# A graph layer and a mixture of experts on one core: the lane columns of the first message list on GpSimd, the second list earlier

## What is computed

```
x = x + gnn(layernorm(x))                     # x: 625 x 512
    h_self = n @ W_self.T + b_self
    H[r]   = n @ W_rel[r].T + b_rel[r]        # r in 0..15, two for each of the 8 relations
    agg[heads] += H[rel, tails]; agg[tails] += H[rel + 8, heads]
    gnn    = relu(h_self + agg)
x = x + moe(layernorm(x))                     # 16 experts, the best 2 for each token
```

## Time and profile before

| what | value |
|---|---|
| median of three runs | 734.15 us |
| the profiled execution, its own time | 737.15 us |
| its span, first to last instruction | 735.4 us |
| TensorE busy | 695.0 us (95%) |
| VectorE busy | 617.0 us (84%) |
| ScalarE busy | 500.8 us (68%) |
| GpSimd busy | 307.4 us (42%) |
| mean granted TensorE clock | 0.98 |
| graph layer, from the trace | 0 to about 404 us |

### The profile page before, as it was taken

How to read it: one execution, slowest core, us unless ns; L and a number is a source line. 1 busy time by engine, 2 the same in 40 slices (tenths; PEclk the granted TensorE clock), 3 DMA queues, 4 the chain that set the end, 5 groups by cost and what they waited for, 6 DMA issues and landing times. The chain is left out here.

```text
span 735.4 us, 10603 instructions
## 1 busy us (share of the span) xinstructions
PE 695.0 (95%) x3210; PEld 546.5 (74%) x3210; DVE 617.0 (84%) x1204; ACT 500.8 (68%) x717; POOL 307.4 (42%) x279
## 2 busy tenths in 40 slices
PE   4999989999998989999997899999999999999993
PEld 4777766777776767777765688888888888888882
DVE  8899978997997757777775899999998999999990
ACT  3555466774675757877556498888877888888860
POOL 3000077752777577776771033322234223333201
PEclk9999999999999999999999899999999999999997
DMA  8347588884988888997767989999999999999932
GB/s 244 124 143 270 176 264 293 302 273 149 305 288 275 268 288 273 302 310 211 226 203 252 353 318 349 398 407 394 401 369 369 367 402 372 363 395 372 371 106 29
DMA packets 54436, 212.75 MB, mean 289 GB/s; under 512 B 9753, under 2 KB 10150, under 8 KB 39158
## 3 DMA queue, kind: packets, MB, share of 16 engines
q1 hardware_dynamic: 34998, 153.85, 55.5%
q0 software_dynamic: 19392, 58.35, 27.3%
HBM read 184.36 MB, written 27.80 MB: 289 GB/s over the span
## 5 line engine op out<-in xcount | busy, mean ns | idle before, releaser
L400 POOL DMA_INDIRECT rows_sb<-h_dram,row_of x190 | 210.9, 1110 | 170.4 <-DVE row_of L544 83.8
L554 DVE TENSOR_TENSOR rows_lo<-rows_sb,rows_hi 128x512 fp32r<-128x512 f32 x175 | 119.8, 685 | 53.6 <-ACT rows_hi L692 53.3
L825 PE MATMUL p_h<-g_hi_sb,xt_hi_whole 128*125 128x512 f32 x320 | 129.6, 405 | 1.1 <-ACT p_h L686 0.8
L826 PE MATMUL p_h<-g_lo_sb,xt_hi_whole 128*125 128x512 f32 x320 | 127.6, 399 | 0.0
L827 PE MATMUL p_h<-g_hi_sb,xt_lo_whole 128*125 128x512 f32 x320 | 127.5, 398 | 0.0
L692 ACT CAST rows_hi<-rows_sb 128x512 fp32r<-128x512 f32 x175 | 99.2, 617 | 29.3 <-DMA rows_sb<-h_dram,row_of 27.1
L677 ACT COPY h_whole<-p_h 125x512 f32<-125x512 f32 x80 | 46.9, 586 | 89.9 <-PE p_h L827 89.9
L1190 POOL DMA_INDIRECT tokens<-token_dram,rows_of_tokens x15 | 21.7, 1444 | 171.2 <-ACT rows_of_tokens L1479 131.9
L859 PE MATMUL p_sum<-rows_hi,seg_hot 128*125 128x512 f32 x175 | 72.7, 416 | 8.6 <-DVE rows_lo L554 8.2
L1243 DVE TENSOR_TENSOR u_lo_sb<-stage_up,u_hi_sb 128x2048 fp32r<-128x2048 f32 x34 | 76.4, 2285 | 1.0
L1243 DVE TENSOR_TENSOR d_lo_sb<-stage_down,d_hi_sb 128x2048 fp32r<-128x2048 f32 x32 | 71.8, 2286 | 3.1 <-ACT d_hi_sb L1464 3.0
(11 more groups left out here) (291 smaller groups left out, 1308.8 us busy)
## 6 DMA issues: line engine op xcount, KB each, us to landing
stage_up<-in_L_ffn_up_w SPq DMA_DIRECT2D x34, 1024.0 KB, 8.2
stage_gate<-in_L_ffn_gate_w SPq DMA_DIRECT2D x32, 1024.0 KB, 8.7
stage_down<-in_L_ffn_down_w SPq DMA_DIRECT2D x32, 1024.0 KB, 7.7
h_dram<-h_whole SPq DMA_DIRECT2D x80, 224.0 KB
stage_up<-in_L_gnn_W_rel SPq DMA_DIRECT2D x16, 1024.0 KB, 8.0
x_whole<-in_L_gnn_b_rel SPq DMA_DIRECT2D x16, 256.0 KB, 9.5
rows_sb<-h_dram,row_of POOLq DMA_INDIRECT x190, 4.9
h_dram<-h_whole SPq DMA_DIRECT2D x80, 26.0 KB
```

The source lines that it names most:

```text
L400: q.indirect_dma_start(rows_sb[:, b % ROWS], None, h_dram[0:1 + made(n) * TP], bass.IndirectOffsetOnAxis(ap=row_of[:, b:b + 1].bitcast(U32 ...
L554: v.tensor_tensor(rows_lo[:, b % PARTS], rows_sb[:, b % ROWS], rows_hi[:, b % PARTS].bitcast(F32), ALU.subtract).then_inc(part_lo, 1)
L825: m.matmul(o, xt_hi[:, dc, at], wt_hi_sb[:, 1 - j % 2, dc], start=(by_matmul and dc == 0), stop=False, skip_group_check=True)
L826: m.matmul(o, xt_hi[:, dc, at], wt_lo_sb[:, 1 - j % 2, dc], start=False, stop=False, skip_group_check=True)
```

## The change

1. GpSimd makes the 85 `lane_hot` columns of list 0, in a loop that stands between its constants and its first gather. Ahead of it is a wait on a new semaphore, `placed`, which VectorE increments when `lane[:, d]` is made. GpSimd waits for `list_taken` as VectorE does, and increments `lanes_made` once for each five columns.
2. VectorE leaves `lane_hot` out for list 0 and makes `told_hot` alone.
3. TensorE's `list_chunk` waits for `lanes_made` too, for list 0.
4. The table of columns changes. List 0: 6.5 columns a product from i = 4. List 1: 5 a product in 19 to 22, 1.5 in 23 to 37, 6 in 38 to 42, 2 from 43. `told_of(1)` and `places(1)` move three products ahead, to i = 17 and 18.

```
-LISTS = ((4, 5.5), (24, 3))
+LISTS = (((4, 18, 6.5),), ((19, 23, 5), (23, 38, 1.5), (38, 43, 6), (43, 58, 2)))
...
+        placed, lanes_made = sem("placed"), sem("lanes_made")
...
-                begin, each = LISTS[d]
-                return max(0, min(EC, int(each * (i - begin))))
+                n = 0
+                for begin, end, each in LISTS[d]:
+                    n += each * (max(begin, min(i, end)) - begin)
+                return min(EC, int(n))
...
                 pool.wait_ge(spare_cleared, 64)
+                pool.wait_ge(placed, 1)
+                for c in range(EC):
+                    n, k = c // HOT, c % HOT
+                    if k == 0 and n >= HOT_SETS:
+                        pool.wait_ge(list_taken, n - HOT_SETS + 1)
+                    i = q.tensor_scalar(lane_hot[:, n % HOT_SETS, k], slot_iota[:], lane[:, 0, c:c + 1], None, ALU.is_equal)
+                    if k == HOT - 1:
+                        i.then_inc(lanes_made, 1)
                 for b in range(BLOCKS):
...
-                    v.scalar_tensor_tensor(lane[:, d], nth, -float(P), place, ALU.mult, ALU.add)
+                    v.scalar_tensor_tensor(lane[:, d], nth, -float(P), place, ALU.mult, ALU.add).then_inc(placed, 1)
...
-                    v.tensor_scalar(lane_hot[:, n % HOT_SETS, k], slot_iota[:], lane[:, d, c:c + 1], None, ALU.is_equal)
+                    if d:
+                        v.tensor_scalar(lane_hot[:, n % HOT_SETS, k], slot_iota[:], lane[:, d, c:c + 1], None, ALU.is_equal)
...
-                    if i == 20:
+                    if i == 17:
                         told_of(1)
...
-                    if i == 21:
+                    if i == 18:
                         places(1)
...
                     pe.wait_ge(list_hot, nth + 1)
+                    if d == 0:
+                        pe.wait_ge(lanes_made, n + 1)
```

More of the change, by code:

```diff
@@ L142, in build @@
         round_sems = range(steps.num, logits_full.num + 1)
-        assert len(round_sems) == 54 + OUTS + BIAS_ROWS
+        assert len(round_sems) == 56 + OUTS + BIAS_ROWS
         ln2_stored, gap_ready, exp_ready = sem("ln2_stored"), sem("gap_ready"), sem("exp_ready")
```

## The result

The changed kernel takes **746.86 us**, the median of 4 runs (745.60 to 749.01), against 734.22 for the kernel before (4 runs). The ratio is 1.017, with a 95% interval from 1.0135 to 1.0205. It is slower by 12.6 us; the forecast was 729.0, the range went up to 746, and the sign was wrong. The profiled execution took 748.01 us, with a span of 746.3; the spans differ by 10.9 us (735.4 before).

What follows compares the result with a forecast made beforehand. TensorE, busy 95% of the span, was taken as the bound, with 9.4 us lost around the lists. Terms -4.0 - 3.5 + 2.3 = -5.2 us took 734.15 to 729.0 us; the range was 722.5 to 746.

Steps and rivals of the forecast that it cites:

- GpSimd's column, x = 0.60 us: List 0: each of GpSimd's 85 lane columns takes 0.60 us, which loses 2.3 us.
- The bounds of 0.31 and 0.89: List 0: lowest and highest time in us of one GpSimd column, the highest if all is in turn.
- the cast of 0.73 us: GpSimd's cast at 7.30 us, 0.73 long where its neighbour took 0.18, read as GpSimd held once by VectorE.
- the pair that had looked undisturbed: VectorE's two-input instruction at 6.65 us ran its usual 0.25 beside a GpSimd cast (6.51 to 6.80).
- The formula for the lateness of the last chunk: List 0's end: loss is the larger of 50.9+55x-81.6 and 30.4+85x-81.6 us, x being one GpSimd column's time.
- The gains of 4.0 and 3.5 us: TensorE's stands and slow clock: 4.0 us won among the first messages, 3.5 from a thinner list 1 beside messages.
- the rival of no change: Gathers stay the bound: the next late landing eats the 1.9 us lead, gains 2 and 1.5, 733.0 us; chance 0.20.
- The stands near 100 to 124: TensorE's two 1.8 us waits for gathered rows; with more lead, 5.4 us including slow clock become about 1.4.
- VectorE at 38 to 42: List 1 at 6 columns a product: VectorE 0.2 us behind in each of five products, counted as nothing.
- VectorE's 85 columns: List 0, 35 to 88 us: 13.6 us leave VectorE, by itself worth nothing since TensorE did not wait there.
- The rival of turns: List 0, 50 to 82 us: GpSimd and VectorE take turns, 751 to 757 us, 742 at partial x; chance 0.28.
- The signs named for "wrong": Column step above 0.69 us, products 8 to 17 over 3.6 us apart, or stands remaining among the first messages.

Runs made afterwards that it cites:

- e12: The change in full, but with list 1's old columns (3 a product from 24 on): 772.65 us, ratio 1.0219 to the kernel before.
- e13: The same kernel as e12 run again, the change in full with list 1's old columns: 746.73 us, interval of the ratio 1.0104 to 1.0194.

## Why the prediction was wrong

By its own steps:

- **GpSimd's column, x = 0.60 us: this step failed.** The price by itself was right: 0.58 was measured beside an idle VectorE, 0.57 was worked out from the earlier trace rows. What failed is the choice to put the contention at 0.03 us, "because `told_hot` and `w_rest` fill only part of a product and VectorE was not held". It was 0.16: the mean is 0.736. Of it 0.10 is `told_hot`, shown by the kernel without it. VectorE was held too, by 50 ns for each `told_hot`. The bounds of 0.31 and 0.89 held it, and of the two rows on contention the cast of 0.73 us in the earlier trace rows pointed the right way; the pair that had looked undisturbed did not.
- **The formula for the lateness of the last chunk was right; what it leaves out is the clock.** 50.9 + 55x would put the last column's end at 91.4 with x = 0.736, and 30.4 + 85x puts it at 93.0. Measured were 92.77 and the chunk at 92.91, so the second, larger term decides. It gives a loss of 30.4 + 62.6 - 81.6 = 11.4 us in place of 2.3. The chunk at 92.91 is 11.3 us behind its 81.6. The fall of the clock behind it, 3.4 us at half speed, is in no term, and product 19 came 13.7 us later than before. The first gather came 12.1 us late in place of 0.5 sooner. That a late chunk "holds the products, their stores and so the first gather" was said in words and is what happened: the first gather waited for a store, and with list 0 to product 19 it started 8.6 us sooner. In the kernel without `told_hot` the formula gives 30.4 + 53.8 + 0.9 (its waits for a buffer) - 81.6 = 3.5 us, and its first gather is 5.3 us late.
- **The gains of 4.0 and 3.5 us: the second step that failed.** The profile has 2.1 us less over the two pieces that hold list 1, of 7.5. In the table without GpSimd's lanes there is no gain at all, but 7 us of loss. For the 4.0, the lead itself came as forecast: the first message is computed 9.0 us behind the first gather (104.42 to 113.41), where it was 7.0 (92.26 to 99.31). But the step from this lead to the stands was wrong: 0.75 and 2.86 us with a fall of the clock are no less than 1.83 and 1.82 with one. That a lead of 2 us would be eaten is what the rival of no change had said. Where the table stands with VectorE's own lanes, the idea that 20 columns ahead of the first message are work "that had to be done anyway" fails too. VectorE is full in list 0 there, so the preparations that are moved ahead make list 0's last chunks and the first gather later (3.1 us of delay in the kernel with early preparations alone). In the change itself VectorE has room, and no chunk of list 0 waited for it. For the 3.5, a thinner list beside the messages did not win: spread alone, it cost 3 us.
- **The stands near 100 to 124 were a lack of lead: right.** Two more products ahead of the first message remove both, and win 6 us. That is 5.7 us of lead more, where the change gave 2.0. Lead is not all of it: with the new table and list 0 to product 19 it was 11.0 us, and two stands of 1.25 and 1.57 near 121 to 123 came all the same.
- **VectorE at 38 to 42, counted as nothing: right.** None of the chunks behind these products waited. What is left of list 1's stand is 1.16 us, at the last chunk behind product 49, and 1.16 in the repeated run. From 220 to 240 the change has 1.0 us more busy time and the full clock (1.8 us), so 2.8 of the 4.0; but from 180 to 220 it loses 1.8 again (37.85 busy, before 39.68).
- **VectorE's 85 columns, worth nothing: right.** With all of them on GpSimd, list 0 is no sooner and the total is that of before.

The numbers follow: 729.0 + (11.4 - 2.3) + 7.5 = 745.6, against 746.9 measured, with the gains at nothing. That this comes so near is in part luck. By the experiments the table and the early preparations cost 6 to 7 us, where this sum has 0, and the rate with GpSimd's pace costs 6.5 where it has 11.4. The rival of turns had its threshold right (slower from x = 0.69, by over 0.5% from 0.74). But at x = 0.736 it gave 738.1, since it kept the gains; to get to 742 and beyond it had needed x = 0.78. It was also the nearest in mechanism. The signs named for "wrong" all came: a mean step above 0.69, the first gather far behind 95, products 8 to 17 4.3 us apart and not 3.6 (50.36 to 88.75), `told_hot` above 0.40, stands left among the first messages.

What stays open: why the spread of list 1 costs 3 us, and whether it still does so in the change. Where list 0 ends at product 19 with the new table, the first gather is 3.5 us late, and the two pieces up to gather 90 take 88.8 and 71.1 us, where they took 86.6 and 70.1; single executions differ by several us. The rate of 6.5 with the preparations at their old place was not tried: `told_of(1)` works in a buffer that the gathers write, and would then stand behind the first of them.

## What to carry to other kernels

Before work is given to an idle engine, price it beside what the busy engine does at that time: 0.58 us alone was 0.74 in company, and 85 such differences were more than the slack. Then look at what stands behind the late result in its consumer's queue: with the same slow columns, list 0's chunks two products later made the first gather 8.6 us sooner and the kernel 6.5 us faster, since no product whose store it awaited stood behind the last of them. A part that costs nothing beside other stands can have a price once they are gone, as GpSimd's columns did (5.5 us). Where messages stand for their gathers, move the start of the messages first; that one number won 6 us, which a new table of columns did not.

## What the runs showed of the hardware

- A GpSimd tensor-scalar instruction on 125 x 128 fp16 values takes 0.592 us at the least and repeats every 0.58 us. Beside VectorE's `told_hot` it took 0.76 us, and one took 1.32 beside two instructions of 128 x 512 fp32 values with two inputs. The 85 `told_hot` beside them took 50 ns more each.
- The lower clock does not follow each stand. It fell for 3.4 us within 1 us of the end of the stands of 3.11, 3.17 and 2.86 in the change, and of the one of 1.82 in the kernel before, but not at that of 1.83 there. In the repeated run of the change the same stands of 3.11 and 3.17 had 6.8 us of lower clock each (a mean of 0.95 from 24 to 90 us and of 0.66 from 90 to 100). Nor did it fall at the one of 1.64 in the change, the one of 2.58 in the kernel with GpSimd's lanes, or the one of this row, of the kernel with three columns of five, whose clock from 24 to 100 us was 1.00:

```profile
84.00 0.56 PE L866 MATMUL p_list<-told_whole,lane_whole 125*128 125x180 f16 x5 [2.20 <-DVE told_whole L544]
```

- The same kernel can be slower for a while: the kernel before took 762 us beside e12, and 734 beside e13 eight minutes later, on the chip of the same number. Why is not known. Only kernels that ran side by side may be compared.
